# Four copies of the router's columns instead of sixteen in the first two batches of a fused attention and mixture-of-experts kernel

## What is computed

```python
x = x + tanh(g_xattn) * einsum("emk,enk->emn", quant_rows(layernorm(x)), quant_blocks(ctx))
n = layernorm(x)
probs = softmax(n.reshape(2048, 512) @ Wg)            # the router: 8 columns
gate_vals, expert_idx = top_k(probs, 2)
# each expert takes the first C = 640 rows that chose it, in row order
h = relu(einsum("ecd,edf->ecf", dispatched, w1))
expert_out = einsum("ecf,efd->ecd", h, w2)
x = x + tanh(g_ffn) * combine(gate_vals, expert_out)
```

## Time and profile before

| | us |
|---|---|
| median of 3 runs | 865.96 |
| lowest, highest | 865.66, 866.23 |
| profiled execution, whole | 871.1 |
| its span, first to last instruction | 869.2 |
| TensorE matmul busy in it | 807.9 (93%) |
| VectorE busy | 600.4 (69%) |
| ScalarE busy | 357.5 (41%) |
| first matmul of the experts, from the span's start | 162.97 |
| mean granted clock of TensorE | 0.981 |

### The profile page before, as it was taken

One profiled execution on the slowest core, in us unless ns is written; L12 is line 12 of the kernel. 1 busy time (PEld: TensorE's weight loads), 2 busy tenths in 40 slices (PEclk: granted clock), 3 DMA queues, 4 the chain that ended last, 5 costly groups with the idle time before them and its releaser, 6 DMA issues.

```text
span 869.2 us, 12186 instructions
## 1 busy us (share of the span) xinstructions
PE 807.9 (93%) x4297; PEld 386.9 (45%) x4298; DVE 600.4 (69%) x958; ACT 357.5 (41%) x586; POOL 227.2 (26%) x219
## 2 busy tenths in 40 slices
PE   0598996699999999999999999999999999999996
PEld 0444665344444444444444444444444444444442
DVE  6999988277667785778577667766775678565430
ACT  4897994343504351434241424251425143404310
POOL 3133131665332043004400430033103310332010
PEclk9999997699999999999999999999999999999998
DMA  8704336695647375638442745263627372612000
GB/s 303 279 1 152 138 128 233 163 194 95 121 124 276 102 118 163 237 97 189 160 170 94 148 165 207 97 145 135 239 97 133 132 256 97 125 45 61 1 27 23
DMA packets 79289, 123.17 MB, mean 142 GB/s; under 512 B 43390, under 2 KB 43406, under 8 KB 75168
## 3 DMA queue, kind: packets, MB, share of 16 engines
q1 hardware_dynamic: 68032, 93.33, 35.8%
q0 software_dynamic: 10944, 29.51, 12.2%
q10 hardware_dynamic: 288, 0.00, 0.0%
HBM read 96.53 MB, written 18.95 MB: 133 GB/s over the span
## 4 chain that ended last, share of the span: by engine, by line
PE 85%; DVE 8%; issue 3%; ACT 2%; DMA 1%; another core or an unknown queue 1%; POOL 0%; SPq 0%; ACTq 0%; DVEq 0%; POOLq 0%
PE mm L787 38%; PE mm L857 38%; PE mm L583 4%; PE mm L827 2%; PE mm L766 2%; DMA w_stage<-in_ctx 1%; DVE region L1256 1%; DVE bn L1193 1%; DVE region L1207 1%; DVE region L1260 1%; DVE w_stage L1256 1%; DVE region L1278 0%; ACT region L1009 0%; DVE region L1302 0%
## 5 line engine op out<-in xcount | busy, mean ns | idle before, releaser
L857 PE MATMUL mm<-region,w_split 128*128 128x512 f16 x1536 | 335.0, 381 | 6.6 <-ACT region L1009 6.1
L787 PE MATMUL mm<-region 128*128 128x512 f16 x1536 | 335.8, 379 | 0.0
L857 PEld LDWEIGHTS mm<-region,w_split 128*128 128x128 f16 x1536 | 150.6, 98 | 189.6 <-issue 9.0
L787 PEld LDWEIGHTS mm<-region 128*128 128x128 f16 x1536 | 148.8, 98 | 181.3 <-issue 4.2
L1131 ACT ACTIVATE region<-mm 128x512 f16<-128x512 f32 x128 | 76.4, 597 | 312.4 <-PE mm L857 298.1
L1562 DVE SCALAR_TENSOR_TENSOR region<-mm,region 128x512 f16<-128x512 f32 x128 | 88.5, 692 | 119.7 <-ACT region L1131 113.7
L507 POOL DMA_INDIRECT out<-region,back_now x40 | 65.1, 1628 | 168.7 <-DVE region L1575 141.6
L1565 DVE SCALAR_TENSOR_TENSOR region<-w_stage,w_scale,region 128x512 f16<-128x512 f32 x128 | 96.2, 751 | 0.0
L1134 ACT ACTIVATE region<-w_stage,w_scale 128x512 f16<-128x512 f32 x128 | 91.2, 712 | 0.0
L1362 DVE SCALAR_TENSOR_TENSOR w_split<-w_stage,w_scale,w_split 128x2048 f16<-128x2048 f32 x32 | 74.0, 2349 | 3.4 <-ACT w_split L893 1.8
L1349 DVE TENSOR_REDUCE top<-w_stage 128x1 f32<-128x512 f32 x112 | 76.0, 678 | 0.0
(11 more groups left out here) (189 smaller groups left out, 577.9 us busy)
## 6 DMA issues: line engine op xcount, KB each, us to landing
w_stage<-in_L_ffn_w SPq DMA_DIRECT2D x64, 1024.0 KB, 5.3
region<-in_x SPq DMA_DIRECT2D x4, 1024.0 KB, 13.2
x_split<-region SPq DMA_DIRECT2D x8, 512.0 KB, 2.9
out<-region SPq DMA_DIRECT2D x4, 1024.0 KB, 5.7
w_stage<-in_ctx SPq DMA_DIRECT2D x2, 1024.0 KB, 11.6
region<-in_ctx SPq DMA_DIRECT2D x2, 1024.0 KB, 15.0
region<-x_split,row_next POOLq DMA_INDIRECT x40
region<-out,row_next POOLq DMA_INDIRECT x40
```

What stands on the lines that cost most here:

```text
L787: mm = pe.matmul(mm2[s % 2][:, :], hidden[:, hh, f, s * P:(s + 1) * P], w2_split[:, wh, f, :], start=(f == 0 and hh + wh == 0), stop=(f == ...
L857: mm = pe.matmul(products(f), w1_split[:, wh, k, f * P:(f + 1) * P], xT[:, xh * KD + k, 0:WIDE], start=(k == 0 and wh + xh == 0), stop=(k ...
```

## The change

The routers of group 0, the tiles of the first two batches, repeat the eight columns four times instead of sixteen: 32 columns stream and are written instead of 128. Those of the groups 1 and 2 keep 128. The number of instructions, their order on every engine, their weight loads and all waits stay the same.

```diff
+FEW_COPIES = 4
...
                     bank = mm1[0][:, 1, :] if g >= 2 else spare_ps
+                    copies = FEW_COPIES if g == 0 else COPIES
                     for k in range(KD):
-                        mm = pe.matmul(bank[:, i * E:(i + COPIES) * E], xnT[:, m, k, :],
-                                       wg_sb[:, k, :].unsqueeze(1).broadcast_to([P, COPIES, E]),
+                        mm = pe.matmul(bank[:, i * E:(i + copies) * E], xnT[:, m, k, :],
+                                       wg_sb[:, k, :].unsqueeze(1).broadcast_to([P, copies, E]),
                                        start=(k == 0), stop=(k == KD - 1), skip_group_check=True)
```

## The result

The changed kernel takes 867.73 us (median of 16 executions, 866.44 to 869.99), the kernel before beside it 865.98 us (16 executions, 864.89 to 867.01): +1.75 us, a ratio of 1.0025 with a 95% interval of 1.0019 to 1.0032. It is slower by a little more than 0.2%. The forecast was 867.2 us, with 865.5 to 868.9 us as its range. One execution of the kernel before (1249.28 us, beside e5_again) and one of e2_batch0 (3036.58 us) were disturbed and stand in no figure here.

The account below looks back on a forecast made before the run. The experts' dense matmuls bound the kernel from 162.97 us, so delays in the preparation reach the end in full. Router gain -0.05 us plus clock loss 1.3 us gave +1.25 us: 865.96 to 867.2 us, range 865.5 to 868.9 us.

Parts of the forecast that it names:

- Step 1: Narrowed routers still start 110 ns apart, paced by weight loads; about 0.05 us gained on the chain's last 8.
- Step 2: The other 56 narrowed router instructions, ahead of waits for VectorE and ScalarE: being faster would bring nothing.
- Step 3: Fewer columns make TensorE's clock fall to half once, near 114 us, delaying the attention matmuls: 1.3 us lost.
- the clock falls once, near 114 us: The main forecast, around the second batch's last router tile: 867.2 us, own range 866.5 to 868.5 us, chance 0.50.
- rival A: The clock holds because the array stays busy as long; only -0.05 us is left: 865.9 us, chance 0.33.
- rival C: Two clock falls, first near 105 us (0.6 us), then at 115 us: 868.2 us, up to 869.5 us; chance 0.12.
- The middle price of 1.3 us: Cost of one half-clock stretch near 114 us, between 0.9 us (partly off the chain) and 1.67 us (all on it).
- Step 4: At the experts' half-clock start the 1.3 us delay may end as 0.65 or 2.3 us; 1.3 us taken, neither.
- D: Narrow routers do run faster and the clock holds: up to -0.66 us, 865.3 us, chance 0.05.

Follow-up runs that it names:

- e5_again: The changed kernel once more, no edit, against the kernel before: 867.70 us, ratio 1.0023.
- e2_batch0: Only the first batch's four router tiles narrowed (32 of the 64 instructions), against the kernel before: 866.70 us, ratio 1.0014.
- e7_copies1: One copy (8 columns) instead of the change's four in the same 64 instructions, against the kernel before: 869.44 us, ratio 1.0037.
- e9_narrow_warm: The changed kernel with 88 unused matmuls between 141 and 158.6 us, against the kernel before: 866.90 us, ratio 1.0006.
- e4_fill: The change plus 8 unused f16 matmuls before the second batch's last router tile, against the kernel before: 867.69 us, ratio 1.0012.
- e3_batch1: Only the second batch's four router tiles narrowed (32 of the 64 instructions), against the kernel before: 868.86 us, ratio 1.0028.
- e6_copies8: Eight copies (64 columns) instead of the change's four in the same 64 instructions, against the kernel before: 865.75 us, ratio 1.0006.
- e8_warm_start: The kernel before plus 88 unused matmuls in TensorE's idle stretches between 141 and 158.6 us, against the kernel before: 865.00 us, ratio 0.9990.
- e10_warm_again: e8_warm_start repeated, the kernel before plus 88 unused matmuls, against the kernel before: 865.38 us, ratio 0.9990.

## Why the prediction was right, and where it was not

**Step 1 held.** 111 ns against the 110 ns taken, with 32 columns and again with 8. From the last router tile to the transpose behind it passes 0.89 us instead of 0.97 us, so the gain is 0.08 us and not 0.05 us.

**Step 2 held.** In the profile after, the attention of the last batch still waits for VectorE and the last tile for ScalarE's copy; the idle time ahead of it grew from 1.07 us to 1.20 us. With a fall near 105 us the first 32 of the other 56 instructions do come onto the chain (e7_copies1, e9_narrow_warm).

**Step 3 had the right cause, and was wrong in place and number.** The clock does fall because of the columns, and the price of one fall at the last tile was foreseen well: 1.67 us by the earlier trace rows, 1.67 us in e5_again. Three things were missed. First, "the clock falls once, near 114 us" and rival A were put as two states of the kernel with a chance each, and both happen, in different executions of one program: the profile on record has no fall, e5_again has it. Second, the stretch near 105 us, which I had given to rival C with 0.12 and only together with a fall at 114 us, is as real: in e4_fill, which up to its filler is the change, and in e7_copies1 the fall stands there alone. It costs 2.1 us (e7_copies1), not rival C's 0.6 us, because it lasts 6.8 us. Third, a fall can last 6.8 us instead of 3.4 us; that costs 3.34 us at 115 us (e3_batch1). Why one lasts twice as long as another was not tried apart. The middle price of 1.3 us, taken for one fall that is partly off the chain, stands in truth for a mixture of 0, 1.7, 2.1, 3.3 and 3.8 us, and that it comes near the median's is in part luck. The forecast of +1.25 us was 0.5 us short of the median's +1.75 us and 0.8 us short of the mean's +2.07 us, and the range held it. By the prediction's own chances a median above 867.7 us had 0.27 and one between 864.2 and 867.7 us had 0.71; the 867.73 us are just in the less likely part, and the interval from 1.0019 leaves "no change" out.

**Step 4 named the right cases, but they differ from execution to execution.** The row of before had the right length and the wrong place: the experts start at 158 us and not at 163 us, and the half clock from there lasts 2.7 to 5.9 us in the profiles without fillers, 3.9 us in that of before. A later start gave back 1.31 us of its 1.91 us in e5_again, 0.95 us of 3.85 us in e3_batch1 and nothing of 2.68 us in e7_copies1, each beside the profile after. That it is neither in the median agrees with e9_narrow_warm, where the start is at the full clock and the change costs 1.5 us, against 1.75 us with the half clock; but the 1.5 us are known to about 1 us only, so this is not shown. And a late start isn't only paid by TensorE: GpSimd's list of 42 us runs beside it, which I did not look at.

**The rivals.** A is what the profile on record shows, by the prediction's own sign (1.00 throughout 96 to 141 us), and is no more than some of the executions; as a theory of the clock, that the recorded busy time holds it, it fell with e4_fill's 3.28 of 3.30 us. C happened, in part of the executions and in e9_narrow_warm's profile as described. Its upper end of 869.5 us doesn't follow from step 4: with 2.3 us of delay half of the other 1.1 us makes 868.8 us. Whether transposes count for the clock was not tried apart, nor whether it is what streams or what is written that tells in a narrower router. D fell by the 111 ns of e7_copies1.

**What stays open.** Why the clock falls in one execution and not in the next of the same program, and what decides between one stretch and two. The work is the same; only the moment of the change differs from trace to trace (68.0 us before, 68.9 us after, and no fall there at all in e3_batch1, e4_fill, e6_copies8, e8_warm_start, e9_narrow_warm and e10_warm_again). Of the change's eleven executions at 0.983, 867.0 to 867.8 us, one has a trace, e5_again's with its one fall of 3.4 us; that the others are like it is likely and not shown. And those of 869 to 870 us have none.

## What to carry to other kernels

A float32 matmul with a fresh 128x128 weight load costs 111 or 112 ns here whether 8 or 128 columns stream, so columns up to 128 are nearly free, and in this kernel no profile with all of them has a fall in that stretch: padding can be worth more than it looks, and taking it away may cost without any instruction growing. Look for the places where light work stands between two heavy blocks on the chain, and price them with a half-clock stretch of the same trace. When the clock is in play take several profiles, or the mean clock of each execution, because one profile shows one outcome; and compare the profiled time with the median first: 5 us more was mostly a delay in that execution, and one that moved the numbers I used.

## What was not expected of the hardware

- The clock fell after 3.3 us in which TensorE's matmul and weight-load columns both read 3.28 us busy (e4_fill). What ran were float32 matmuls with 32 columns and transposes.
- One program has executions with 3.4 us of half clock at a place and others without any there (e5_again and the first profile of the change), and the cost goes by the place: nothing at 68 us, 1.67 us at 116 us (e5_again), 3.34 us for twice the length at 115 us (e3_batch1).
- At the half clock the router tile takes 1.78 us instead of 1.05 us (e3_batch1): the weight load slows too, one from 192 ns to 338 ns.
- 88 matmuls that compute nothing, put into idle stretches, made the first expert's first product 2.7 us shorter (41.61 against 44.35 us) and the whole 0.1% faster, less than the 2.7 us, in part because TensorE then waits for VectorE, behind GpSimd's lists.
